# A linear-attention and FFN layer on one core: other call orders on all five engines, same operations and buffers

## The reference

```python
q, k, v = x @ Wq, x @ Wk, x @ Wv;  g = sigmoid(x @ Wf + bf)
state = state * gt[..., None] + vt[..., None] * kt[..., None, :]   # per head, 16 heads of 8x8
out_t = einsum('bhij,bhj->bhi', state, qt)                         # a scan over the tokens
out = layernorm(out) * gamma + beta
x = layernorm(x + (out * silu(x @ Wg)) @ Wout)
h = silu(x @ W1.T * s1) * (x @ W2.T * s2)                          # 512 wide
h = gelu(h @ H1.T * s);  h = gelu(h @ H2.T * s)
x = layernorm(x + h @ W3.T * s3)
```

## Time and profile before

| | us |
|---|---|
| median of 3 runs (511.7 to 512.26) | 511.95 |
| the profiled execution | 511.54 |
| its span, first to last instruction | 509.6 |
| PE busy | 496.3 (97%) |
| DVE busy | 448.7 (88%) |
| ACT busy | 406.4 (80%) |
| POOL busy | 311.7 (61%) |

### The profile page before, as it was taken

How to read it: one execution, slowest core, us unless ns; L and a number is a source line. 1 busy time by engine, 2 the same in 40 slices (tenths; PEclk the granted TensorE clock), 3 DMA queues, 4 the chain that set the end, 5 groups by cost and what they waited for, 6 DMA issues and landing times.

```text
span 509.6 us, 7946 instructions
## 1 busy us (share of the span) xinstructions
PE 496.3 (97%) x2528; PEld 382.4 (75%) x2528; DVE 448.7 (88%) x708; ACT 406.4 (80%) x839; POOL 311.7 (61%) x363
## 2 busy tenths in 40 slices
PE   8999999999999999999999999999999999999995
PEld 5576777777878777786877777786877777787995
DVE  4999989999999899998999999899999999993352
ACT  5775968888887888978797788988778987868863
POOL 0751848668392766848385765938477683929432
PEclk9999999999999999999999999999999999999998
DMA  6899999953994497689969675799719483710001
GB/s 244 205 267 236 255 263 241 230 125 84 275 221 104 104 246 177 154 195 249 259 183 234 142 185 125 186 222 244 196 51 235 130 194 94 183 25 1 23 23 44
DMA packets 21500, 87.33 MB, mean 171 GB/s; under 512 B 2512, under 2 KB 3280, under 8 KB 13520
## 3 DMA queue, kind: packets, MB, share of 16 engines
q1 hardware_dynamic: 21168, 86.46, 67.9%
q10 hardware_dynamic: 288, 0.33, 0.2%
HBM read 74.72 MB, written 12.06 MB: 170 GB/s over the span
## 4 chain that ended last, share of the span: by engine, by line
PE 48%; POOL 17%; DVE 13%; issue 13%; ACT 7%; DMA 1%; POOLq 0%; DVEq 0%; ACTq 0%
PE F L2342 26%; POOL h1lo L479 5%; PE front L2243 5%; POOL h2lo L479 5%; PE back L2441 4%; DVE KJ L1590 3%; DVE QJ L1597 2%; POOL KJ L541 2%; DVE QJ L1605 2%; PE ps_v L2243 2%; PE back L2328 2%; PE back L2227 1%; DMA out<-res 1%; POOL rstd_o L511 1%; POOL y L553 1%
## 5 line engine op out<-in xcount | busy, mean ns | idle before, releaser
L903 ACT ACTIVATE h<-F,cols 128x512 f32<-128x512 f32 x120 | 80.7, 686 | 17.0 <-PE F L2342 16.5
L479 POOL TENSOR_TENSOR h1lo<-h,h1hi 128x512 fp32r<-128x512 f32 x60 | 76.5, 1291 | 12.8 <-ACT h1hi L896 12.7
L547 POOL TENSOR_TENSOR QJ<-QJ 128x512 f32<-128x512 f32 x14 | 18.0, 1284 | 108.0 <-DVE QJ L1605 108.0
L479 POOL TENSOR_TENSOR h2lo<-h,h2hi 128x512 fp32r<-128x512 f32 x60 | 77.2, 1309 | 4.9 <-ACT h2hi L896 4.7
L1590 DVE TENSOR_TENSOR_SCAN KJ<-g,carry,KJ 128x512 f32<-128x512 f32 x64 | 78.5, 1263 | 0.9 <-ACT carry L829 0.8
L1590 DVE TENSOR_TENSOR_SCAN KJ<-g,KJ 128x512 f32<-128x512 f32 x64 | 74.3, 1202 | 1.6 <-POOL KJ L528 0.7
L1597 DVE TENSOR_TENSOR QJ<-QJ,KJ 128x1024 f32<-128x1024 f32 x60 | 72.9, 1237 | 0.2
L2342 PE MATMUL F<-h2hi,whi 128*128 128x512 f32 (+1 forms) x256 | 71.6, 415 | 0.8 <-ACT h L903 0.7
L2342 PE MATMUL F<-h1hi,whi 128*128 128x512 f32 (+1 forms) x256 | 68.9, 410 | 1.6 <-DVE h L1654 1.3
L2342 PE MATMUL F<-h1lo,whi 128*128 128x512 f32 (+1 forms) x256 | 67.4, 400 | 0.2 <-POOL h1lo L479 0.2
L2342 PE MATMUL F<-h2lo,whi 128*128 128x512 f32 (+1 forms) x256 | 65.7, 397 | 0.0
(11 more groups left out here) (184 smaller groups left out, 935.9 us busy)
## 6 DMA issues: line engine op xcount, KB each, us to landing
KJ<-qk_bounce SPq DMA_DIRECT2D x30, 1024.0 KB, 9.9
QJ<-qk_bounce SPq DMA_DIRECT2D x30, 1024.0 KB, 11.0
qk_bounce<-qk SPq DMA_DIRECT2D x30, 256.0 KB, 4.6
x_in<-in_x SPq DMA_DIRECT2D x16, 256.0 KB, 11.4
xT<-in_xT SPq DMA_DIRECT2D x15, 256.0 KB, 11.5
out<-res SPq DMA_DIRECT2D x15, 256.0 KB, 3.3
wraw<-in_wffn SPq DMA_DIRECT2D x2, 1024.0 KB, 6.6
wraw<-in_wffn SPq DMA_DIRECT2D x2, 256.0 KB, 4.6
```

Of the source, the lines that this page charges most:

```text
L479: e.tensor_tensor(h_lo[layer][:, t, :w], h[:, t, :w], h_hi[layer][:, t, :w].bitcast(f32), ALU.subtract).then_inc(lo_done[layer], 1)
L547: e.tensor_tensor(first, first, other, ALU.add).then_inc(add_gp_done, 1)
L903: e.activation(dst[:, t, :WIDTH[n]], F[t][:, :WIDTH[n]], ACT.Gelu, scale=scale[t]).then_inc(gelu_done[layer], 1)
```

## The change

Nothing is added or removed: all five lists are permutations of themselves (of the calls, GpSimd's 246 move at 102 places, DVE's 470 at 190, ACT's 548 at 418, PE's 730 at 353, SP's 146 at 116), and the functions, waits and buffers are unchanged. Lines cut from the diff, one or two for each of the places that are spoken of:

```diff
@@ -318,150 +318,150 @@
...
+            send(12, 1)
+            load_x(10)
...
             store(13)
+            store_half(0)
             store(14)
-            store_half(0)
             store_half(1)
@@ -582,31 +582,31 @@
             lo(2, 0, 2)
+            rstd_of(1, "1")
             lo(2, 0, 3)
-            rstd_of(1, "1")
@@ -990,480 +990,480 @@
...
+            center_w3()
             tanh(2)
...
+            silu_gate(4)
+            g_of_tanh(4)
+            save_carry(3)
+            x1_hi(2)
             gelu(2, 1, 0)
...
+                last_half(0)
                 tail_hi_products(2, 1, 3, low_parts)
```

More of the change, by code:

```diff
@@ L347, in _ @@
             fetch(2, 0, 1)
+            fetch(3, 0, 0)
+            load_x(2)
             fetch(3, 1, 0)
+            load_xT(5)
             send(4, 1)
             fetch(3, 1, 1)
[L351 to L358, removed]
             fetch(4, 1, 0)
             fetch(4, 1, 1)
+            fetch(3, 0, 1)
+            send(4, 0)
+            load_xT(6)
+            load_x(3)
             fetch(4, 0, 0)
@@ L376, in _ @@
             send(6, 1)
+            load_xT(8)
+            load_x(4)
             fetch(5, 0, 1)
@@ L598, in _ @@
             lo(2, 1, 1)
+            rstd_of(2, "1")
             lo(2, 1, 2)
-            rstd_of(2, "1")
             lo(2, 1, 3)
+            add_gp(3)
             kv_gp(4, 6)
-            add_gp(3)
-            kv_gp(4, 7)
             lo(1, 2, 0)
             lo(1, 2, 1)
+            lo(1, 2, 2)
             rstd_of(3, "o")
-            lo(1, 2, 2)
             lo(1, 2, 3)
+            kv_gp(4, 7)
             rstd_2(1)
@@ L632, in _ @@
             add_gp(5)
+            kv_gp(6, 6)
             lo(1, 4, 0)
+            kv_gp(6, 7)
+            rstd_of(5, "o")
             lo(1, 4, 1)
-            rstd_of(5, "o")
             lo(1, 4, 2)
@@ L688, in _ @@
             lo(2, 7, 2)
+            rstd_of(8, "1")
             lo(2, 7, 3)
-            rstd_of(8, "1")
-            rstd_2(6)
             add_gp(9)
             lo(1, 8, 0)
+            kv_gp(10, 6)
+            rstd_2(6)
+            rstd_of(9, "o")
             lo(1, 8, 1)
-            rstd_of(9, "o")
-            kv_gp(10, 6)
             lo(1, 8, 2)
@@ L781, in _ @@
             add_gp(15)
+            rstd_2(12)
             lo(1, 14, 0)
@@ L1093, in _ @@
             silu(2, 0)
-            silu_gate(4)
+            norm_2(0)
+            silu(2, 1)
             copy_v(4)
-            silu(2, 1)
             hi(1, 2, 0)
@@ L1128, in _ @@
             hi(1, 3, 0)
+            silu_gate(5)
+            g_of_tanh(5)
             hi(1, 3, 1)
-            silu_gate(5)
             silu(3, 2)
             silu(3, 3)
-            g_of_tanh(5)
             hi(1, 3, 2)
+            square(2)
             save_carry(4)
@@ L1332, in _ @@
             silu(9, 3)
+            save_carry(10)
+            hi(1, 9, 2)
             copy_k(12)
-            hi(1, 9, 2)
+            g_of_tanh(11)
             hi(1, 9, 3)
@@ L1393, in _ @@
             silu(11, 2)
+            save_carry(12)
             hi(1, 11, 1)
@@ L1537, in _ @@
             tail_gelu(2, 1, 3)
+            norm_2(14)
+            save_carry(15)
             norm_half()
@@ L1996, in _ @@
             hmul(8, 3)
-            kv(10, 0)
-            kv(10, 1)
             scan(10, 0)
             scan(10, 1)
-            kv(10, 2)
-            qs(10, 0)
-            scan(10, 2)
-            residual_1(9)
-            scan(10, 3)
-            stats_1(9)
+            kv(10, 1)
+            scan(10, 2)
+            scan(10, 3)
+            qs(10, 0)
+            residual_1(9)
+            stats_1(9)
+            kv(10, 2)
             scan(10, 4)
```

944 lines of the change are left out of this document (464 added, 480 removed).

## The result

| | before | after |
|---|---|---|
| median (lowest to highest), us | 512.05 (511.7 to 512.82), 6 runs | 516.15 (515.52 to 517.53), 6 runs |
| ratio | | 1.0081, 95% interval 1.0068 to 1.0095 |
| the profiled execution | 511.54 | 516.42 |
| its span | 509.6 | 514.5 |
| `up_hi(0, 0)` | 43.99 | 45.45 |

The forecast was 511.2, a gain of 0.7 us, with a range to 514.6. The change costs 4.1 us by the medians, 4.9 by the two profiled executions.

The account below looks back on a forecast made before the run. PE was taken as nearly full in the middle stretch, open 0.6 us a batch. Terms +0.1 - 0.6 + 0.5 - 0.8 + 0 + 0.1 sum to -0.7 us, giving 511.2 us on the median, range 507.5 to 514.6.

Parts of the forecast that it names:

- the low parts: GpSimd's low parts in the other batches: fewer `kv_gp` against added small work, taken at 0, bounds -3 and +3 us.
- SP's list: SP's DMA order: only `load_x` issued later was considered, bounded at 0 if its transfer is in time.
- the order of the last stores: Tail: `store_half(0)` goes out earlier, ending nothing; with `last_half(0)` moved ahead, the tail was +0.1 us, bounds 0 and +1.
- Rival 1: GpSimd's order delays low parts in batches 4, 5, 7, 8: 3.7 us slower, 514.9 us; chance 0.18.
- PE's slack: In the 14 middle batches PE stands open for 8.6 us, 0.6 a batch, capping what any order can give.
- The overlaps: DVE and GpSimd operations on two SBUF operands meeting: parting them gives -0.8 us, bounds -6.2 and 0.
- Batch 0: Layers 1 and 2 of batch 0, with `center_w3` and `rstd_of` moved: -0.6 us net, bounds -1.3 and +0.5.
- Batch 1: Two more ACT table loads from `silu_gate(4)`, mostly hidden behind an earlier norm: +0.5 us, bounds 0 and +1.8.
- The start: ACT's `sum_low_parts(2)` ahead of `affine(0)`, against calls leaving PE and DVE there: +0.1 us, bounds -0.5 and +1.5.
- Rival 2: `load_x(10)` and `load_x(4)` issued behind waiting sends, so x lands late: +3.8 us, 515.0 us; chance 0.07.
- The signs: Profile checks named beforehand, among them products by Q at most 1.3 us and `up_hi(2, 0)` at most 1 us later.

Follow-up runs that it names:

- e11: The kernel before with only SP's first 13 calls in the changed order: 512.95 us, ratio 1.0021 to before.
- e2: The changed kernel with `store(14)` back ahead of `store_half(0)` on SP, one swap: 514.1 us, ratio 1.0037 to before.
- e8: The kernel before with one swap on SP, `store_half(0)` ahead of `store(14)`: 513.05 us, ratio 1.0014 to before.
- e12: The kernel before with one GpSimd call moved, `kv_gp(7, 6)` ahead of `add_gp(6)`: 516.05 us, ratio 1.0075 to before.
- e6: e2's kernel with `add_gp` back ahead of `kv_gp` on GpSimd at four places (6, 8, 12, 13): 512.99 us, ratio 1.0016 to before.
- e7: e2's kernel with `silu_gate(4)` on ACT back behind `silu(2, 0)`, two table loads fewer: 515.13 us, ratio 1.0058 to before.
- e1: The changed kernel with SP's first 13 calls in the order of before: 515.85 us, ratio 1.0073 to before.
- e9: The changed kernel with the edits of e1, e2 and e6 together: 513.0 us, ratio 1.0018 to before.
- e10: e9 with `norm_2(14)` on ACT ahead of `tail_gelu(2, 1, 0)` again: 513.1 us, ratio 1.0017 to before.

## Why the prediction was wrong

The forecast was -0.7 us and the runs show +4.1.

**The steps that failed** are three terms put at 0 or near it: the low parts (below, the largest), SP's list and the order of the last stores. The last two are sentences that cost nothing. "SP. The order shows `load_x` issued later: bounded at 0 if its transfer is in time": I priced one kind of call of SP's list and left out the other moves in it. The head of the list, with `load_xT(2)` behind a call that waits, costs PE 0.4 us alone (e11) and 0.8 beside the other changed lists. And "`store_half(0)` goes out earlier, which ends nothing": it goes out no earlier, and the call that it is moved past goes out 12 us later, into the last store. In the changed kernel's profile the end is longer by 1.2 us, and it shrinks by 0.9 when the swap is undone (e2); alone (e8) it is 0.9 by the timed runs and not shown by the trace. A call that is moved past a waiting one gets its wait.

**The low parts.** "I take 0, bounds -3 and +3" counted what stands among the low parts and nothing of what stands ahead of `add_gp`. The loss in the middle, 1.9 us from batch 0 to 14, came from there, and not by the 1.29 us of an instruction but by a wait for a DMA. None of the earlier trace rows shows it, but the trace of before has both ends: that half of K landed at 196.23 us and `add_gp(6)` started at 194.37, so a product by that half ahead of it had to hold it. Moved alone, the call costs 2.8 us (e12); putting four back takes 1.57 us out of the middle (e6 against e2: 1.63 less 0.06). Rival 1 had the engine and the sign, and 3.7 us, but by added work in batches 4, 5, 7 and 8, which the ledger doesn't show.

**PE's slack** was also put too low. The sum of the first paragraph has 560 short products between the two `up_hi`; the trace has 528 (the last product of batch 13 comes later), and 1116 instead of 1120 of the FFN. That makes 393.1 us and not 397.5, and PE stands open for 13.0 us, 0.93 a batch, which fits the 0.95 and 1.11 that the prediction has by batch. Rival 1 was priced with the 0.6.

**The overlaps.** Taken at -0.8 with a bound of -6.2: with the four `kv_gp` back, PE's middle stands within 0.1 us of the kernel before. So PE gained nothing in the net; no run parts the overlaps alone, so their share isn't shown apart. There was also less to gain than 6.2 us: DVE and GpSimd are lengthened by 3.2 us before and 2.4 after. The late starts were no such thing. ACT's row for `gated_y` at 119.44 is

```profile
118.59 0.77 ACT L870 ACTIVATE y<-back,cols 128x512 f32<-128x512 f32 x1
```

which ends at 119.36: GpSimd had its operand 0.08 us before it started, and the end of DVE's product at 119.46 was chance. All eight `gated_y` that waited before, and all six after, start 0.08 us behind ACT's end, also where DVE's product had ended long ago (236.97 behind 236.89, DVE's product at 236.08). The stretched pairs don't look like sharing either. The operation that starts second is the one that is lengthened, in all eleven cases by the time that the two overlap less 0.13 to 0.16 us: the product at 60.84 overlaps `gated_y` (60.23 to 61.54) by 0.70 and is longer by 0.56, the low part at 61.47 overlaps that product by 1.15 and is longer by 0.99. That fits a second one that waits for the first, with its wait counted as busy time.

**Batch 0.** -0.6 was forecast; -0.1 came, 1.46 to 1.32 in the ledger at `up_hi(1, 0)`. The fourth low part of layer 1 starts as far behind `up_hi(0, 0)` as before, 11.9 us (11.8 before): taking `center_w3` out of ACT's way gave nothing, since `rstd_of(1, "o")` ahead of it on GpSimd waits for DVE's statistics:

```profile
55.79 0.20 POOL L508 TENSOR_TENSOR rstd_o<-mv_o,eps 128x4 f32<-128x4 f32 x1 [0.75 <-DVE mv_o L1615]
...
57.33 1.30 POOL L479 TENSOR_TENSOR h1lo<-h,h1hi 128x512 fp32r<-128x512 f32 x1
```

**Batch 1.** +0.5 for the table loads: the wait is there with that size (e7: 0.55), and what I missed is that the batch gives it back. ACT's timeline after shows two loads without a gap ahead of them:

```profile
98.78 1.28 ACT L843 ACT_TABLE_LOAD   x1
100.07 0.60 ACT L843 ACTIVATE gate<-front 128x512 f32<-128x512 f32 x1
...
101.80 1.28 ACT L903 ACT_TABLE_LOAD   x1
```

The load took 1.28 us and the next activation began 0.01 later, in agreement with the earlier trace rows. The Trainium skill, page "ScalarE: Activation LUTs", section "What ACT_TABLE_LOAD costs", adds a drain of about 1.38 us to each switch; no run here shows it.

**The start.** `sum_low_parts(2)` ahead of `affine(0)` cost nothing that can be seen: with the old head of SP's list and the changed orders elsewhere it is 33.3 us from the first scan to `up_hi(0, 0)` in e1, e9 and e10, 0.3 less than before. So +0.1 for this part was 0.4 too high by the columns less the clock's part, inside its bounds; the SP part beside it was missing.

**Rival 2**, a late x, did not come: in the changed kernel no wait of L1644 is ended by a DMA, and `load_x(10)` landed 4.9 us after its issue.

**The signs.** Two of them spoke against what happened: a product by Q took 2.21 us (at 63.46, at most 1.3 was forecast), and `up_hi(2, 0)` came 29.4 us behind `up_hi(1, 0)`, 1.4 more than before (at most 1 was forecast). From `up_hi(0, 0)` to `up_hi(14, 0)` it is 409.1 us, 3.0 more than before (1.9 in the ledger, which compares the same product).

The sum as the two profiles have it: the clock of the execution 1.04, the start 0.42 (SP's head 0.8, the rest -0.4), the middle 1.91 (four `kv_gp`), the last batch 0.37, the end 1.17, together 4.9. By the medians the change costs 4.1, and e9, which undoes the head, the four `kv_gp` and the last stores, recovers 3.15.

## What to carry to other kernels

In a kernel with lists of calls, price each call by what it waits for and by who stands behind it on its engine, DMA lists first: a product that waits for a transfer must not stand ahead of one that the busiest engine waits for. A load or a store moved behind a call that waits gets that wait too, and at the ends of the program nothing gives it back. Compare the traces of two orders by the bottleneck engine's lost time at the same product; busy shares of 97% and 97% hid 4 us.

## What the runs showed of the hardware

- Of an operation on two SBUF operands of DVE and one of GpSimd that overlap, the one that starts second is lengthened by the overlap less 0.13 to 0.16 us, in all eleven cases before and after. The trace shows it as a longer operation and not as idle time. Eight before, three after; PE gained nothing in the net.
- TensorE ran its first products at half rate (0.85 us for a projection record, later 0.43) up to a moment that differed from execution to execution: from 4.42 to 7.60 us in the twelve traces of the table and of before, with the same work of PE from 1.45 us on. Each us more costs half a us at the start of the FFN. The clock column reads 1.00 there; the distance of two starts shows the rate. Where it lay in the runs without a profile isn't on record, but they can carry this scatter too: differences below 0.5 us from one kernel to another are not settled by 5 to 12 runs.
- The last store, 128 KB, took 2.87 and 3.47 us to land with 256 KB issued 1.3 us ahead of it (after, e1), and 1.94 to 2.40 in the six kernels with the other order and the same lists else. With the lists of before it took 1.70 to 2.20 (before, e11, e12), and 2.09 with 256 KB issued 0.9 us ahead (e8).
